# A two-layer graph network on one core: the last layer's bias added by one transfer for each stream, and seven orders changed on TensorE, ScalarE and VectorE

## The chip, the core and the metric

The kernel runs on one core of a Trainium2 chip. The metric is the time of the device in microseconds (us). A core has TensorE (matrix products), VectorE, ScalarE, GpSimd (POOL) and SyncE (SP). Each takes its instructions strictly in its program's order, and they are tied together by semaphores alone: an instruction that waits holds up all that stands behind it on its engine. Transfers (DMAs) are issued by SP and by POOL. The inputs and outputs are float32.

## The reference

`x` is (64, 128, 128): 64 batches of T = 128 nodes and D = 128 features. `adj` is 128 x 128. Cut to what matters:

```python
h = maximum(layernorm(x), 0)
# first layer: two graph convolutions, then windowed LSTMs
h = relu(adj @ (h @ Wg0 + bg0));  h = relu(adj @ (h @ Wg1 + bg1))      # for each batch
for p in 1, 2, 3, 4:               # skips: windows of p nodes through an LSTM, its last
    last = lstm_last(Wih[p-1], Whh[p-1], bih[p-1], bhh[p-1], windows(h, p))
    h[:, p-1::p, :] = last         # state replaces the window's last node
x = x + h
# last layer
h = maximum(layernorm(x), 0)
out = diag(adj) * (h @ W[0]) + triu(adj, 1) @ (h @ W[1]) + tril(adj, -1) @ (h @ W[2]) + bias
x = x + out
```

## The kernel before

The 64 batches are taken in 4 groups of 16 (`GROUPS`, `G`), and a group in 2 streams of 8 batches (`STREAMS`, `HB`). The LSTM of a group is a list of 22 units (`UNITS`, line 48), each one step of one window length for one stream: units 0 to 3 have p = 1, 4 to 7 p = 2, 8 to 13 p = 3, 14 to 21 p = 4. Even units are stream 0, odd ones stream 1. A unit's gates are I, C, O at the first step of a window and I, C, F, O after it. Every product is split in three passes for precision (line 596 high x high, 597 low weights x high, 605 high weights x low data; 624, 625 and 628 likewise for the recurrent product). The pass with the low data needs what VectorE writes last for a unit (`unit_low`, lines 1101 to 1107).

For each unit ScalarE makes the gates (line 915) and the tanh of the cell (930); VectorE makes the cell (`unit_cell`, 1029), the hidden state (`unit_hidden`, 1070) and its low part. PSUM has 8 banks, 4 for each stream, one for each gate.

The last layer of a group is computed during the LSTM of the next group. Its operands come turned around by transfers: POOL issues, for each stream, a 512 KB transfer that adds the LSTM's result to the turned x (line 469), then two transfers of 256 KB that add minus the mean (476), then the reciprocal deviation (`rstd`, 425), and after both streams one transfer of 1024 KB that adds the bias to the 16 batches of `X` (484, semaphore `bias_in`). The means themselves go through DRAM by SP (`spread_means`, 381). The last group is different: it has no such transfers, and its bias is added on POOL and VectorE.

A table written by hand (`START`, `START_F`, `STEADY`, `LATE`, lines 95 to 118) places the last layer's pieces between the LSTM's gates: a key (k, m) is "in unit k before its gate m", or after its gates if m is their number. The pieces on TensorE are VALUE n (the three products of batch n), SUM q (the two adjacency products of a quad of 4 batches) and a wait FORGET n. They use the bank of gate F, so F's products wait for what `START_F` names. On ScalarE `TURN_AT` places `turn_up(q)` (the relu of the turned x of quad q), and a VALUE is copied from PSUM there too. On VectorE three steps are placed by `START_MID` (after the unit's cell and before its hidden state), `START_BETWEEN` (after the hidden state) and `START_LATE` (after the low part): LOW q (`turn_down`, the low part of the turned x), OWN q (`add_own`, the diagonal term into `X`) and ADD q (`add_out`, the SUM into `X`). A number of -1 means quad 3 of the group one further back, and is left out if there is none. So in group 1 nothing with -1 runs; in groups 2 and 3 it does. `LN_STATS_AT` places the first layer norm's statistics of the next group.

OWN waits for the bias to be in `X`:

```python
        def add_own(g, q, lo=0, hi=PACK):
            dve.wait_ge(value_sb, G * g + q * PACK + hi)
            ...
                dve.wait_ge(bias_in, 16 * ((QUADS * g + q) // QUADS + 1))     # line 1170
```

Here g is the group whose last layer is done, one less than the group whose LSTM runs; QUADS = 4, HBANKS = 2, and a transfer adds 16 to its semaphore. `START_MID = {0: ((OWN, -1),), ...}` has OWN -1 in unit 0, between cell and hidden state.

Of the kernel before, what the change touches and what calls it, by code (L numbers as in the profile page):

```python
# [62 lines left out]
def last_unit(k, s):  # L63
# [37 lines left out]
         (8, 0): (Piece(VALUE, 8, 0, (VALUE, 7)),), (8, 3): (Piece(SUM, 1, 1, (FORGET, 7)),),  # L101
         (9, 3): (Piece(VALUE, 9, 0, (VALUE, 8)),), (10, 3): (Piece(VALUE, 10, 1, (SUM, 1)),),
# [43 lines left out]

LN_STATS_AT = {3: range(0, 3), 5: range(3, 5), 6: range(5, 9), 10: range(9, 12), 11: range(12, G)}
LN_COMBINE_AT = 11
# [11 lines left out]
def program(nc, x_tbd, x_dbt, adj_t, adj_diag, wg0, bg0_col, wg1, bg1, wih_t, whh_t, bih_t, bhh_t, w_l1, bias, bias_row, out_tbd):  # L160
    with ExitStack() as ctx:
# [116 lines left out]
        xt_summed = [sem(f"xt_summed{s}") for s in range(STREAMS)]  # L278
        xt_centred = [sem(f"xt_centred{q}") for q in range(QUADS)]
        means_out = [sem(f"means_out{s}") for s in range(STREAMS)]  # L280
        bias_in = sem("bias_in")
        turn_mm = sem("turn_mm")
# [70 lines left out]
        def _(sp):  # L353
# [34 lines left out]
            def store(i, quads):  # L388
                for q in quads:
                    pieces = END_PIECES if i == GROUPS - 1 and q == LAST else ((0, PACK),)  # L390
                    for n, (lo, hi) in enumerate(pieces):
                        if on_pool(i, q):
                            sp.wait_ge(pool_shifted, q + 1)
                        elif i == GROUPS - 1:
                            sp.wait_ge(shifted_x, shifts_to(q))
                        else:
                            sp.wait_ge(bias_in, 16 * (i + 1))
                        sp.wait_ge(out_ready, QUADS * i + q + 1 + n)
                        part = slice(i * G + q * PACK + lo, i * G + q * PACK + hi)
                        sp.dma_start(out_tbd[:, part, :], X[:, part, :]).then_inc(stored, 16)  # L400
# [16 lines left out]
        def _(pool):  # L417
# [42 lines left out]
            def group(i):  # L460
                if i == 0:
                    for s in range(STREAMS):
                        rstd(VE1, var1, 2 * (QUARTERS + s + 1), RS1, rs1, HB * s, HB * s + HB)
                else:
                    rstd(VE1, var1, 2 * (QUARTERS + i + 2), RS1, rs1, 0, G)
                pool.wait_ge(xt_in, 16 * (i + 1))
                for s in range(STREAMS):
                    pool.wait_ge(lstm_step, STEPS * i + STEPS_BEFORE[LAST_OF[s] + 1])
                    pool.dma_start(turned_stream(s), HF[:, s, :, :, :].rearrange("p c t e -> p (c t e)"),
                                   accum_op=ALU.add).then_inc(xt_summed[s], 16)  # L470
                for s in range(STREAMS):
                    pool.wait_ge(xt_summed[s], 16 * (i + 1))
                    pool.wait_ge(means_out[s], 16 * (i + 1))
                    for h in range(HBANKS):
                        part = slice(h * PACK * T, (h + 1) * PACK * T)
                        pool.dma_start(turned_stream(s)[:, part], MEANS[i, s, part].rearrange("(a n) -> a n", a=1).broadcast_to(
                            [128, PACK * T]), accum_op=ALU.add).then_inc(xt_centred[HBANKS * s + h], 16)
# [5 lines left out]
                part = slice(i * G, (i + 1) * G)  # L483
                pool.dma_start(X[:, part, :].rearrange("t b d -> t (b d)"), bias_row.rearrange("(a n) -> a n", a=1).broadcast_to(
                    [T, G * D]), accum_op=ALU.add).then_inc(bias_in, 16)

# [16 lines left out]
        def _(pe):  # L503
# [47 lines left out]
            def unit(k, i, plan):  # L551
# [24 lines left out]
                for m, q in enumerate(gates):  # L576
# [21 lines left out]
                    if j == 0 and p > 1 and plan is None:  # L598
                        continue
                    if prev is None and m == 0:  # L600

                        pe.wait_ge(h_low, 2 * HBANKS * i + HBANKS * (s + 1))
                    if j == 0 and p > 1 and m == 0:
                        pe.wait_ge(h_out, LOWS * i + prev + 1)
                    mm = pe.matmul(dst, WIH[:, p - 1, cols], x_low, start=False, stop=(j == 0))  # L605
                    if j == 0:
# [7 lines left out]
                if j > 0:  # L614

                    pe.wait_ge(lstm_step, STEPS * i + STEPS_BEFORE[prev] + STEPS_OF[prev])
                    for q in gates:
                        if i == GROUPS - 1 and k == LAST_OF[1] and q == gates[-1]:

                            pe.wait_ge(gate_act, GATES * i + GATES_BEFORE[LAST_OF[0]] + len(LATER_STEP))  # L620
                            transpose_h(0, i, range(PACK))
                        dst = bank(s, q)[:, 0:n]
                        cols = slice(q * D, q * D + D)
                        pe.matmul(dst, WHH[:, p - 2, cols], SH[:, s, 0:n], start=False, stop=False)  # L624
                        pe.matmul(dst, WHL[:, p - 2, cols], SH[:, s, 0:n], start=False, stop=False)  # L625
                        if q == gates[0]:
                            pe.wait_ge(h_out, LOWS * i + prev + 1)
                        pe.matmul(dst, WHH[:, p - 2, cols], SL[:, s, 0:n], start=False,  # L628
                                  stop=True).then_inc(gate_mm, 1)
# [176 lines left out]
        def _(act):  # L806
# [164 lines left out]
        def _(dve):  # L971
# [190 lines left out]
            def add_own(g, q, lo=0, hi=PACK):  # L1162
# [69 lines left out]
            def units(i, more, plan):  # L1232
                for k in range(len(UNITS)):
# [127 lines left out]
```

## Time and profile before

| what | value |
|---|---|
| median of 3 runs | 403.95 us (403.22 to 404.17) |
| the profiled execution's own time | 402.31 us |
| its span | 400.1 us |
| TensorE busy | 390.5 us (98%) |
| VectorE busy | 335.8 us (84%) |
| ScalarE busy | 281.1 us (70%) |
| POOL busy | 63.9 us (16%) |
| moved by DMA | 23.78 MB |

Busy and idle times are those of one execution. The groups' LSTMs begin at about 24, 107, 200 and 297 us of the span. A row of a timeline gives the start and the duration in us, the engine, the line, output <- inputs with shapes, and in brackets how long the engine was idle before it and what ended that. In the views matmuls overlap (a 512-column pass is shown as 0.39 us, but one starts every 0.23 us). POOL's rows of an issue last as long as it writes the transfer's descriptors; the data follows.

### The profile page before, as it was taken

To read this page: it belongs to the slowest core of one execution; us is meant where nothing else is said; L and a number is where in the kernel's file an instruction comes from. 1 tells how busy PE (TensorE), PEld (TensorE's weight loads), DVE (VectorE), ACT (ScalarE), POOL (GpSimd) and SP (SyncE) were. 2 spreads that over 40 slices of the span, in tenths; PEclk is the share of its full clock that TensorE was granted. 3 is DMA by queue.
4 is the path that set the end of the run, shared out by engine and by line. 5 is a ranking of instruction groups with operands and counts; after the bars stand their busy time and mean duration, and the time that the engine had idled before them with its cause. 6 is when DMAs were issued, how large, how long until landed. Compare 5 with 4: busy or idle time off the path is not lost.

```text
span 400.1 us, 6501 instructions
## 1 busy us (share of the span) xinstructions
PE 390.5 (98%) x2346; PEld 339.4 (85%) x2346; DVE 335.8 (84%) x868; ACT 281.1 (70%) x555; POOL 63.9 (16%) x65
## 2 busy tenths in 40 slices
PE   7999999999999999999999799999999999999997
PEld 7787889998976889899877579999897788989886
DVE  6569999998998788797997678989798958787897
ACT  4768777875697777776499477676669867667554
POOL 4910200101340003001151000300134000000250
PEclk9999999999999999999999999999999999999999
DMA  7860000005364000204158000030527400000003
GB/s 208 304 252 2 0 0 2 2 0 106 53 93 94 0 28 0 92 41 80 29 80 157 27 2 27 2 131 2 107 27 131 108 0 28 0 28 1 2 1 131
DMA packets 12127, 23.78 MB, mean 59 GB/s; under 512 B 4672, under 2 KB 6080, under 8 KB 10816
## 3 DMA queue, kind: packets, MB, share of 16 engines
q0 software_dynamic: 3024, 9.44, 13.6%
q1 hardware_dynamic: 9072, 13.94, 10.1%
q8 instruction: 18, 0.29, 0.3%
q14 instruction: 13, 0.11, 0.1%
HBM read 16.01 MB, written 4.22 MB: 51 GB/s over the span
## 4 chain that ended last, share of the span: by engine, by line
PE 44%; DVE 29%; DMA 12%; ACT 9%; issue 3%; POOL 2%; SPq 0%; DVEq 0%; POOLq 0%; ACTq 0%
DMA X<-bias_row 8%; PE PS L596 6%; PE PS L605 6%; PE PS L597 6%; PE PS L628 4%; ACT GT L915 4%; PE PS L624 4%; PE PS L625 4%; DMA means<-MINUS 4%; PE PS L666 3%; DVE CS L1058 3%; DVE IC L1040 3%; ACT TC L930 2%; DVE ST L1121 2%; DVE CS L1050 2%
## 5 line engine op out<-in xcount | busy, mean ns | idle before, releaser
L915 ACT ACTIVATE GT<-PS,BG 128x256 f32<-128x256 f32 (+2 forms) x312 | 158.2, 563 | 17.0 <-PE PS L628 14.2
L596 PE MATMUL PS<-HH,WIH 128*128 128x256 f32 (+2 forms) x312 | 106.6, 342 | 2.5 <-DVE X L1182 2.4
L597 PE MATMUL PS<-HH,WIL 128*128 128x256 f32 (+2 forms) x312 | 102.7, 330 | 0.0
L605 PE MATMUL PS<-HL,WIH 128*128 128x256 f32 (+2 forms) x294 | 97.4, 331 | 0.6
L930 ACT ACTIVATE TC<-CS 128x512 f32<-128x512 f32 (+2 forms) x88 | 44.9, 510 | 48.2 <-DVE CS L1058 33.2
L596 PEld LDWEIGHTS PS<-HH,WIH 128*128 128x128 f32 x312 | 58.7, 188 | 12.9 <-DVE HH L1099 4.2
L428 POOL TENSOR_TENSOR RS<-VE,NHALF 128x4 f32<-128x4 f32 (+2 forms) x18 | 34.7, 1926 | 210.0 <-DVE VE L994 140.5
L597 PEld LDWEIGHTS PS<-HH,WIL 128*128 128x128 f32 x312 | 58.8, 188 | 4.0 <-issue 1.2
L605 PEld LDWEIGHTS PS<-HL,WIH 128*128 128x128 f32 x294 | 55.5, 189 | 7.1 <-DVE HL L1107 2.5
L628 PE MATMUL PS<-SL,WHH 128*128 128x256 f32 (+2 forms) x192 | 60.2, 313 | 0.2
L624 PE MATMUL PS<-SH,WHH 128*128 128x256 f32 (+2 forms) x192 | 60.0, 312 | 0.0
L625 PE MATMUL PS<-SH,WHL 128*128 128x256 f32 (+2 forms) x192 | 59.7, 311 | 0.0
L1040 DVE TENSOR_TENSOR IC<-GT 128x256 f32<-128x256 f32 (+2 forms) x48 | 23.8, 496 | 21.7 <-ACT GT L915 21.5
L628 PEld LDWEIGHTS PS<-SL,WHH 128*128 128x128 f32 x192 | 36.2, 189 | 2.2 <-DVE SL L1107 0.8
L624 PEld LDWEIGHTS PS<-SH,WHH 128*128 128x128 f32 x192 | 36.3, 189 | 1.5 <-DVE SH L1099 0.2
L625 PEld LDWEIGHTS PS<-SH,WHL 128*128 128x128 f32 x192 | 36.3, 189 | 1.3
L1095 DVE TENSOR_TENSOR HT<-GT,TC 128x256 f32<-128x256 f32 (+2 forms) x48 | 23.7, 495 | 7.5 <-ACT TC L930 6.5
L1095 DVE TENSOR_TENSOR HF<-GT,TC 128x512 f32<-128x512 f32 (+2 forms) x32 | 18.9, 591 | 8.1 <-ACT TC L930 7.5
L1037 DVE TENSOR_TENSOR CS<-GT 128x512 f32<-128x512 f32 (+2 forms) x40 | 23.8, 596 | 1.8 <-ACT GT L915 1.6
L1107 DVE TENSOR_TENSOR SL<-HT,SH 128x256 fp32r<-128x256 f32 (+2 forms) x48 | 23.9, 497 | 1.5
L1058 DVE TENSOR_TENSOR CS<-IC,CS 128x256 f32<-128x256 f32 (+3 forms) x48 | 23.4, 488 | 1.6
L658 PE MATMUL PS<-WLH,HTH 128*128 128x384 f32 x64 | 23.4, 366 | 1.3 <-DVE HTL L1152 0.6
(99 smaller groups left out, 640.1 us busy)
## 6 DMA issues: line engine op xcount, KB each, us to landing
out_tbd<-X SPq DMA_DIRECT2D x15, 256.0 KB, 2.0
X<-x_tbd SPq DMA_DIRECT2D x3, 1024.0 KB, 12.9
H<-x_dbt SPq DMA_DIRECT2D x3, 1024.0 KB, 6.1
H<-HF POOLq DMA_DIRECT2D x6, 512.0 KB, 4.7
H<-means POOLq DMA_DIRECT2D x12, 256.0 KB, 5.0
X<-bias_row POOLq DMA_DIRECT2D x3, 1024.0 KB, 9.8
WI<-wih_t SPq DMA_DIRECT2D x1, 1024.0 KB, 5.5
X<-x_tbd SPq DMA_DIRECT2D x3, 256.0 KB, 3.5
```

The costliest lines, as they stand in the source:

```text
L428: pool.tensor_tensor(rs[:, lo:hi], ve[:, lo:hi], NHALF[:, lo:hi], ALU.pow).then_inc(done, 1)
L596: pe.matmul(dst, WIH[:, p - 1, cols], x_high, start=True, stop=False)
L597: pe.matmul(dst, WIL[:, p - 1, cols], x_high, start=False, stop=False)
L605: mm = pe.matmul(dst, WIH[:, p - 1, cols], x_low, start=False, stop=(j == 0))
L624: pe.matmul(dst, WHH[:, p - 2, cols], SH[:, s, 0:n], start=False, stop=False)
L625: pe.matmul(dst, WHL[:, p - 2, cols], SH[:, s, 0:n], start=False, stop=False)
L628: pe.matmul(dst, WHH[:, p - 2, cols], SL[:, s, 0:n], start=False, stop=True).then_inc(gate_mm, 1)
L915: act.activation(GT[:, s, q, 0:n], bank(s, q)[:, 0:n], ACT.Tanh if q == C else ACT.Sigmoid, bias=BG[:, 4 * (p - 1) + q:4 * (p - 1) + q + 1 ...
L930: act.activation(TC[:, s, done:n], CS[:, s, done:n], ACT.Tanh).then_inc(tanh_ready, 1)
L1040: dve.tensor_tensor(IC[:, s, 0:n], GT[:, s, I, 0:n], GT[:, s, C, 0:n], ALU.mult).then_inc(lstm_step, 1)
L1058: dve.tensor_tensor(CS[:, s, half:n], IC[:, s, half:n], CS[:, s, half:n], ALU.add).then_inc(cell_ready, 1)
L1095: dve.tensor_tensor(full, o, tc, ALU.mult).then_inc(lstm_step, 1)
```

## The change

POOL's bias transfer of 1024 KB becomes two of 512 KB, one for each stream, each with a semaphore of its own. That of stream 0 is issued as soon as stream 0's statistics have been taken (`bn2`), ahead of the transfers of the means; that of stream 1 after the second `rstd`. The two transfers of 256 KB of means for each stream become one of 512 KB. The waits are rewritten accordingly, in `store`, `turn_up` and `add_own`. In the tables: VALUE 9 moves from after unit 9's gates to before its gate O; the relu `turn_up(2)` from before unit 6's VALUE 5 copy to after it; ADD -1 in unit 1 from after to before the hidden state; ADD 1 from unit 9 to unit 8; the next group's statistics of batches 0 to 4 from the middle of units 3 and 5 to the end of unit 5. In units 8 and 15 of groups 1 to 3 the low pass of the first gate is issued with that of the second gate; in units 10 and 16 of group 0 and unit 16 of group 3 the same is done for the recurrent low pass.

```diff
-         (9, 3): (Piece(VALUE, 9, 0, (VALUE, 8)),), (10, 3): ...
+         (9, 2): (Piece(VALUE, 9, 0, (VALUE, 8)),), (10, 3): ...
-TURN_AT = {(1, 1): 0, (4, 1): 1, (6, 0): 2, (10, 0): 3}
+TURN_AT = {(1, 1): 0, (4, 1): 1, (6, 2): 2, (10, 0): 3}
-START_BETWEEN = {0: ((LOW, 0),), 1: ((ADD, -1),), 14: ((ADD, 2),)}
-START_MID = {0: ((OWN, -1),), 4: ((LOW, 1),), 5: ((ADD, 0),), 7: ((OWN, 1),), 9: ((ADD, 1),), 12: ((OWN, 2),)}
+START_BETWEEN = {0: ((LOW, 0),), 14: ((ADD, 2),)}
+START_MID = {0: ((OWN, -1),), 1: ((ADD, -1),), 4: ((LOW, 1),), 5: ((ADD, 0),), 7: ((OWN, 1),), 8: ((ADD, 1),), 12: ((OWN, 2),)}
+LOWS_TOGETHER = (8, 15)
-LN_STATS_AT = {3: range(0, 3), 5: range(3, 5), 6: range(5, 9), 10: range(9, 12), 11: range(12, G)}
+LN_STATS_LATE_AT = {5: range(0, 5)}
+LN_STATS_AT = {6: range(5, 9), 10: range(9, 12), 11: range(12, G)}
...
# SP, store
-                            sp.wait_ge(bias_in, 16 * (i + 1))
+                            sp.wait_ge(bias_in[q // HBANKS], 16 * (i + 1))
# POOL, group(i)
+                def stream_bias(s):
+                    pool.wait_ge(bn2, G * i + HB * (s + 1))
+                    part = slice(i * G + s * HB, i * G + (s + 1) * HB)
+                    pool.dma_start(X[:, part, :].rearrange("t b d -> t (b d)"),
+                                   bias_row.rearrange("(a n) -> a n", a=1).broadcast_to([T, HB * D]),
+                                   accum_op=ALU.add).then_inc(bias_in[s], 16)
+                stream_bias(0)
                 for s in range(STREAMS):
                     pool.wait_ge(xt_summed[s], 16 * (i + 1))
                     pool.wait_ge(means_out[s], 16 * (i + 1))
-                    for h in range(HBANKS):
-                        ...                      # two transfers, xt_centred[HBANKS * s + h]
+                    pool.dma_start(turned_stream(s), MEANS[i, s, :]...,
+                                   accum_op=ALU.add).then_inc(xt_centred[s], 16)
                     ...
                     rstd(VE2, var2, 2 * STREAMS * i + 2 * s + 2, RS2, rs2, HB * s, HB * s + HB)
-                pool.wait_ge(bn2, G * (i + 1))
-                ...                              # one transfer for 16 batches, bias_in
+                stream_bias(1)
# TensorE, unit: with a plan, in units 8 and 15
+                    if plan and k in LOWS_TOGETHER and m == 0:
+                        continue
-                    if j == 0 and p > 1 and m == 0:
+                    if j == 0 and p > 1 and m == (1 if k in LOWS_TOGETHER else 0):
                         pe.wait_ge(h_out, LOWS * i + prev + 1)
+                    if k in LOWS_TOGETHER and m == 1:
+                        ...                      # the first gate's low pass, then_inc(gate_mm, 1)
+                        together = (plan is None and k in (10, 16)) or (i == GROUPS - 1 and k == 16)
...
# ScalarE, turn_up
-                    act.wait_ge(xt_centred[q], 16 * (g + 1))
+                    act.wait_ge(xt_centred[q // HBANKS], 16 * (g + 1))
# VectorE, add_own
-                    dve.wait_ge(bias_in, 16 * ((QUADS * g + q) // QUADS + 1))
+                    dve.wait_ge(bias_in[q // HBANKS], 16 * (g + 1))
# VectorE, units, after plan.late
+                    if more and plan and k in LN_STATS_LATE_AT:
+                        stats1(i + 1, LN_STATS_LATE_AT[k])
```

## Rows read from the trace of the kernel before

**Rows 1.** The page's first lines: span, then busy us, share and instructions of TensorE.
```profile
span 400.1 us, 6501 instructions
PE 390.5 (98%) x2346; PEld 339.4 (85%) x2346; DVE 335.8 (84%) x868; ACT 281.1 (70%) x555; POOL 63.9 (16%) x65
```

**Rows 2.** The page's slices: TensorE's granted clock, tenths of full speed.
```profile
PEclk9999999999999999999999999999999999999999
```

**Rows 3.** The page's chain that ended last, shares of the span by line.
```profile
DMA X<-bias_row 8%; PE PS L596 6%; PE PS L605 6%; PE PS L597 6%; PE PS L628 4%; ACT GT L915 4%; PE PS L624 4%; PE PS L625 4%; DMA means<-MINUS 4%; PE PS L666 3%; DVE CS L1058 3%; DVE IC L1040 3%; ACT TC L930 2%; DVE ST L1121 2%; DVE CS L1050 2%
```

**Rows 4.** The same chain in order of time: start us, us, what.
```profile
200.53 5.53 DMA means<-MINUS
...
208.36 1.08 POOL RS L428
209.44 11.82 DMA X<-bias_row
...
305.86 9.80 DMA X<-bias_row
```

**Rows 5.** POOL's timeline, the issues of the means in groups 0, 1, 2.
```profile
104.26 1.76 POOL L476 DMA_DIRECT2D H<-means  x2 [9.55 <-DMA means<-MINUS]
...
206.56 1.80 POOL L476 DMA_DIRECT2D H<-means  x2 [4.81 <-DMA means<-MINUS]
...
302.97 1.96 POOL L476 DMA_DIRECT2D H<-means  x2 [3.39 <-DMA means<-MINUS]
```

**Rows 6.** The page's DMA issues: count, KB each, median us to landing.
```profile
H<-HF POOLq DMA_DIRECT2D x6, 512.0 KB, 4.7
H<-means POOLq DMA_DIRECT2D x12, 256.0 KB, 5.0
```

**Rows 7.** Line 385 alone, the six transfers of 4 KB of means.
```profile
DMA to landing us min/median/max: 3.1/4.6/5.5
```

**Rows 8.** VectorE's timeline, start of groups 2 and 3.
```profile
202.69 0.75 DVE L1173 SCALAR_TENSOR_TENSOR X<-WH,DIAG,X 128x512 f32<-128x512 f32 x1
...
204.61 0.68 DVE L1152 SCALAR_TENSOR_TENSOR HTL<-H,HTH 128x512 fp32r<-128x512 f32 x1
...
205.82 0.68 DVE L1107 TENSOR_TENSOR HL<-HF,HH 128x512 fp32r<-128x512 f32 x1
...
207.87 0.68 DVE L1182 TENSOR_TENSOR X<-PS,X 128x512 f32<-128x512 f32 x1
...
221.36 0.75 DVE L1173 SCALAR_TENSOR_TENSOR X<-WI,DIAG,X 128x512 f32<-128x512 f32 x1 [2.66 <-DMA X<-bias_row]
...
223.23 0.48 DVE L975 BATCH_NORM_STATS2 ST<-X 128x6 f32<-128x128 f32 x2
...
228.07 0.69 DVE L1040 TENSOR_TENSOR IC<-GT 128x512 f32<-128x512 f32 x1 [1.98 <-ACT GT L915]
...
299.56 0.75 DVE L1173 SCALAR_TENSOR_TENSOR X<-WH,DIAG,X 128x512 f32<-128x512 f32 x1
...
315.76 0.75 DVE L1173 SCALAR_TENSOR_TENSOR X<-WI,DIAG,X 128x512 f32<-128x512 f32 x1 [0.16 <-DMA X<-bias_row]
```

**Rows 9.** TensorE's timeline in group 2: VALUE 0, VALUE 1, unit 6's gate F.
```profile
207.01 0.34 PE L658 MATMUL PS<-WLH,HTH 128*128 128x384 f32 x1
...
208.60 0.45 PE L658 MATMUL PS<-WLH,HTH 128*128 128x384 f32 x1 [0.20 <-DVE X L1182]
...
223.37 0.50 PE L596 MATMUL PS<-HH,WIH 128*128 128x512 f32 x1 [2.40 <-DVE X L1182]
```

**Rows 10.** ScalarE's timeline in group 1: `turn_up(0)`.
```profile
109.88 0.62 ACT L851 ACTIVATE HTH<-H 128x512 fp32r<-128x512 f32 x1
```

**Rows 11.** Waits of weight loads: us in total, times, longest.
```profile
PEld PS L605 <- DVE HL L1107: 2.5, 7, 0.4
...
PEld PS L658 <- DVE X L1182: 2.1, 5, 0.7
...
PEld PS L628 <- DVE SL L1107: 0.8, 3, 0.3
```

More of the change, by code:

```diff
@@ L101 @@
          (8, 0): (Piece(VALUE, 8, 0, (VALUE, 7)),), (8, 3): (Piece(SUM, 1, 1, (FORGET, 7)),),
-         (9, 3): (Piece(VALUE, 9, 0, (VALUE, 8)),), (10, 3): (Piece(VALUE, 10, 1, (SUM, 1)),),
+         (9, 2): (Piece(VALUE, 9, 0, (VALUE, 8)),), (10, 3): (Piece(VALUE, 10, 1, (SUM, 1)),),
          (11, 3): (Piece(VALUE, 11, 0, (FORGET, 10)),), (14, 3): (Piece(SUM, 2, 1, (FORGET, 13)),)}
-TURN_AT = {(1, 1): 0, (4, 1): 1, (6, 0): 2, (10, 0): 3}
+TURN_AT = {(1, 1): 0, (4, 1): 1, (6, 2): 2, (10, 0): 3}
 START_F = {6: (SUM, 0), 7: (VALUE, 6), 10: (VALUE, 9), 11: (VALUE, 10), 12: (VALUE, 11)}
-START_BETWEEN = {0: ((LOW, 0),), 1: ((ADD, -1),), 14: ((ADD, 2),)}
-START_MID = {0: ((OWN, -1),), 4: ((LOW, 1),), 5: ((ADD, 0),), 7: ((OWN, 1),), 9: ((ADD, 1),), 12: ((OWN, 2),)}
+START_BETWEEN = {0: ((LOW, 0),), 14: ((ADD, 2),)}
+START_MID = {0: ((OWN, -1),), 1: ((ADD, -1),), 4: ((LOW, 1),), 5: ((ADD, 0),), 7: ((OWN, 1),), 8: ((ADD, 1),), 12: ((OWN, 2),)}
 START_LATE = {4: ((OWN, 0),), 5: ((LOW, 2),), 9: ((LOW, 3),)}
@@ L278, in program @@
         xt_summed = [sem(f"xt_summed{s}") for s in range(STREAMS)]
-        xt_centred = [sem(f"xt_centred{q}") for q in range(QUADS)]
+        xt_centred = [sem(f"xt_centred{s}") for s in range(STREAMS)]
         means_out = [sem(f"means_out{s}") for s in range(STREAMS)]
-        bias_in = sem("bias_in")
+        bias_in = [sem(f"bias_in{s}") for s in range(STREAMS)]
         turn_mm = sem("turn_mm")
@@ L473, in group @@
                     pool.wait_ge(means_out[s], 16 * (i + 1))
-                    for h in range(HBANKS):
-                        part = slice(h * PACK * T, (h + 1) * PACK * T)
-                        pool.dma_start(turned_stream(s)[:, part], MEANS[i, s, part].rearrange("(a n) -> a n", a=1).broadcast_to(
-                            [128, PACK * T]), accum_op=ALU.add).then_inc(xt_centred[HBANKS * s + h], 16)
+                    pool.dma_start(turned_stream(s), MEANS[i, s, :].rearrange("(a n) -> a n", a=1).broadcast_to(
+                        [128, HB * T]), accum_op=ALU.add).then_inc(xt_centred[s], 16)
                     if i > 0:
@@ L481, in group @@
                     rstd(VE2, var2, 2 * STREAMS * i + 2 * s + 2, RS2, rs2, HB * s, HB * s + HB)
-                pool.wait_ge(bn2, G * (i + 1))
-                part = slice(i * G, (i + 1) * G)
-                pool.dma_start(X[:, part, :].rearrange("t b d -> t (b d)"), bias_row.rearrange("(a n) -> a n", a=1).broadcast_to(
-                    [T, G * D]), accum_op=ALU.add).then_inc(bias_in, 16)
+                stream_bias(1)
             for i in range(GROUPS - 1):
@@ L599, in unit @@
                         continue
+                    if plan and k in LOWS_TOGETHER and m == 0:
+                        continue
                     if prev is None and m == 0:
                         pe.wait_ge(h_low, 2 * HBANKS * i + HBANKS * (s + 1))
-                    if j == 0 and p > 1 and m == 0:
+                    if j == 0 and p > 1 and m == (1 if k in LOWS_TOGETHER else 0):
                         pe.wait_ge(h_out, LOWS * i + prev + 1)
+                    if k in LOWS_TOGETHER and m == 1:
+                        first = gates[0]
+                        pe.matmul(bank(s, first)[:, 0:n].rearrange("p (w b) -> p w b", b=HB),
+                                  WIH[:, p - 1, first * D:first * D + D], x_low, start=False, stop=True).then_inc(gate_mm, 1)
                     mm = pe.matmul(dst, WIH[:, p - 1, cols], x_low, start=False, stop=(j == 0))
@@ L625, in unit @@
                         pe.matmul(dst, WHL[:, p - 2, cols], SH[:, s, 0:n], start=False, stop=False)
-                        if q == gates[0]:
+                        if together and q == gates[0]:
+                            continue
+                        if q == gates[1 if together else 0]:
                             pe.wait_ge(h_out, LOWS * i + prev + 1)
+                        if together and q == gates[1]:
+                            first = gates[0]
+                            pe.matmul(bank(s, first)[:, 0:n], WHH[:, p - 2, first * D:first * D + D], SL[:, s, 0:n],
+                                      start=False, stop=True).then_inc(gate_mm, 1)
                         pe.matmul(dst, WHH[:, p - 2, cols], SL[:, s, 0:n], start=False,
@@ L1348 @@
         "bias": a["L1_gnn_bias"],
-        "bias_row": np.broadcast_to(a["L1_gnn_bias"], (G, D)).reshape(G * D),
+        "bias_row": np.broadcast_to(a["L1_gnn_bias"], (HB, D)).reshape(HB * D),
     }
```

## The prediction

> **What bounds the kernel now.** I read the page's busy times first: TensorE is busy 390.5 of 400.1 us [rows 1], so whatever makes TensorE wait is added to the time, and there are at most some 10 us to gain. Its granted clock is at its full level, 2.4 GHz, in every slice [rows 2]. Then the chain of waits: its largest line is the bias transfer, 8% of the span [rows 3], in stretches of 9.80 and 11.82 us [rows 4]. Such a share says that the chain runs through the transfer, not that removing it frees so much: TensorE works beside it. What the transfer costs stands in the timelines. In group 2 VectorE comes to OWN 0 and is idle 2.66 us until the bias has landed [rows 8]; TensorE then finds unit 6's gate F blocked (it waits for ADD 0, behind OWN 0) and is idle 2.40 us [rows 9]. In group 3 the same wait is 0.16 us [rows 8]. So the intended prize is about 2.5 us, and a few tenths elsewhere [rows 11].
>
> **The new wait.** The part that decides is one line of `add_own`, so I follow its index. OWN -1 runs in groups 2 and 3 between cell and hidden state of unit 0, with q = -1 and g = i - 1. Before, (4g - 1) // 4 + 1 is g: it asks for 16g, the bias of the group two back, landed 78 us before in group 3 (221.26 in the chain, OWN -1 at 299.56) [rows 4, 8]. After, -1 // 2 is -1, so it takes the last semaphore, that of stream 1, and asks for 16(g + 1): the second bias transfer of group g itself, which at that time isn't even issued. It is no deadlock: POOL issues that transfer without anything that VectorE has still to do. But VectorE stands at OWN -1, which began at 202.69 and 299.56 without a wait [rows 8], until the landing, which I call T2 and T3. Behind it on VectorE are the hidden state of unit 0, LOW 0, cell 1 and all else; ScalarE finishes the gates of unit 1 and stops at the tanh of cell 1; TensorE does units 0 and 1, SUM -1 and two gates of unit 2, and stops at VALUE 0, at 207.01 before [rows 9], which needs LOW 0. In group 1 there is no OWN -1 and no such wait.
>
> **When the transfer lands.** Before, POOL began to issue the second stream's means at 206.56 and 302.97 [rows 5], two issues in 1.80 and 1.96, so 0.9 for one. After, one issue is left. The chain has 1.08 from the end of the issue to the next one, for the reciprocal deviation [rows 4]. So the second bias is issued at 206.56 + 0.9 + 1.08 = 208.5, and at 302.97 + 1.98 = 304.95. A 512 KB transfer of the same kind lands 4.7 after its issue [rows 6]. Alone it would land at 213.2 and 309.65: the lower bound. Behind the means' 512 KB, issued 2.0 earlier and itself needing 4.7, it is up to 2.7 later: 215.9 and 312.35. The upper bound is the landing of today, 221.26 and 315.66 [rows 4]. I take T2 = 215.5 and T3 = 311.9, near the middle value, since the two transfers share the same engines and the means may be a little late (below).
>
> The Trainium skill, DMA: Bandwidth & Descriptors, section "Anatomy of one DMA — SWDGE (gpsimd) path", fits a transfer issued by GpSimd as 2.0 us plus its bytes at 436 GB/s, which is 3.2 us for 512 KB. The row of this case has 4.7 (these transfers add to what is there), so the measurement is used; by the page's fit both landings would come some 3 us sooner and the sum below would be some 6 us less.
>
> **From the landing to the time.** From OWN -1 at 202.69 VectorE needed until 205.3 to have LOW 0 done (204.61 + 0.68), until 206.5 for the low part of unit 0, and ADD -1 takes 0.6 more when it stands right there, as after the change [rows 8]. VALUE 1 needs ADD -1, so it starts at T2 + 4.5, against 208.60 before: TensorE is late by T2 - 204.1. VectorE is late by T2 - 202.7, which is 1.4 more. Units 0 to 5 leave it nearly no idle time, so that doesn't shrink, but for some 0.4 from ADD -1's new place and the statistics that leave units 3 and 5. At OWN 0 the old wait of 2.66 is gone, as that needs only the first bias transfer, and stream 0's was issued long before. VectorE then carries T2 - 205.8; TensorE, whose 2.40 is gone too, would have T2 - 206.5; the later one decides, since unit 6's gate F waits for ADD 0. Group 2: 215.5 - 205.8 = 9.7. In group 3 the wait at OWN 0 was only 0.16: T3 - 299.56 - 0.16 - 0.4 = T3 - 300.1, which is 11.8. After unit 6 TensorE is the bound, at 98%, and nothing can give the delay back. Sum +21.5.
>
> **The other parts.** (a) The first bias transfer, 512 KB, is issued when stream 0's statistics are done, some 0.5 us before the 4 KB write of the means and in its way. The shortest of these writes takes 3.1, the one beside another transfer 5.53 [rows 4, 7]. That would make stream 0's means up to 2 us late. They were issued at 104.26 in group 1 [rows 5], so the first relu, at 109.88 [rows 10], which now needs the whole 512 KB (4.7 from the issue) [rows 6], has from 0.9 us of cover to 1.1 us of stall. Bounds -0.2 to +1.5, taken +0.5, for group 1 alone; in the others the new stall covers it. (b) Two instead of one low pass behind the wait, in units 8 and 15 and in the recurrent units: at most what stands in the rows, 2.5 + 0.8 [rows 11]; many of these stalls are in other units, so -1.4. (c) ADD 1 one unit earlier, VALUE 9 and the relu of quad 2 moved: VALUE waits for an ADD 2.1 in all [rows 11], a part of it in these places: -0.6. ADD 1 stands behind SUM 1, which is done by then, and VectorE is waiting for a tanh there. (d) The statistics at the end of unit 5 fall into VectorE's idle time of 1.98 us before the cell of unit 6: five at 0.24 each, 1.2, cost nothing; without that cover they would cost as much as they did in units 3 and 5 [rows 8]. (b) and (c) could also bring nothing, or cost a few tenths where the first gate comes later to ScalarE: together between -3.0 and +0.5, taken -2.0. (e) TensorE's idle time in the new stall, from 207.0 to T2 + 2.6, is some 11 us, where the longest shown before a matmul is 2.40 [rows 9]. If its clock falls in it, a 512-column pass takes 0.46 for 0.23 afterwards; 1.4 us of that are covered by VectorE being later. With 4 us at the lower level that is 0.6 a stall: +1 for both; bounds 0 and the rival below.
>
> Sum: 402.3 + 21.5 + 0.5 - 2.0 + 1.0 = 423.3 for an execution like the profiled one. The median of the runs shown is 1.6 above that one (403.95 against 402.31), so **425.0**.
>
> **Rivals.** (1) The stall isn't there: the semaphore is met in time, or something covers it. This is the other side. The point from which it decides is a landing before 202.7, and the issue alone is later than that. Then group 2 gains 2.4, the rest -1.5: 402.3 - 3.9 + 1.6 = 400. For it: all other edits aim at a real wait. Against it: the index above. (2) Splitting doesn't bring the second landing forward: same bytes on the same engines, landing at 221.3 and 315.7 as now. That adds 5.8 + 3.8 = 9.6: 434.6. Against it: 0.5 MB of 1.5 are gone from behind the means, and the stores of finished quads stand still in the stall. (3) TensorE's clock falls and stays low. No row of this trace shows a fall: even after 2.40 us of idleness it is at the upper level [rows 2, 9]. With 12 us at the lower level in each of two stalls it loses 6.0 - 1.4 = 4.6 a stall instead of the 0.5 counted: 433. A rule of the Trainium skill speaks for this one: TensorE: Matmul & The Clock Gate, section "What's actually happening", has 1.2 GHz as the default and says that activity releases it, so an idle TensorE comes back slow.
>
> **How the numbers follow.** Forecast 0.75, rival 1 0.06, rival 2 0.07, rival 3 0.12. The forecast's own bounds: both landings at their lower bound take 2.3 + 2.25 off and (b, c) one more, 419; to the other side 1 us later each, and 1 each from (a) and (b, c), 429. The range that leaves 2 in 10 out takes in part of rivals 2 and 3: 417 to 434. A difference under 0.3% can't be told from none in this kernel. Only rival 1 gives faster or the same: faster 0.05, same 0.01, slower 0.94.
>
> **What would show it.** In the changed kernel's profile: in groups 2 and 3 OWN -1 (line of `add_own`) idle before it by 10 to 13 us, ended by the bias transfer; none in group 1, whose length stays within 1.5 us of before. The hole in TensorE 8 to 12 us before VALUE 0, twice, and its busy share down to about 93%. No idle time before OWN 0. The granted clock in the slices after each hole tells (e) and rival 3. The issue and landing of the second bias transfer tell T2, T3 and rival 2. The prediction is wrong if OWN -1 doesn't wait, or if later units make up the delay, which would show as group 2 being less than 8 us longer with the stall in place.

## The result, and the profile after

The changed kernel takes **423.4 us** (median of 4 runs, 422.63 to 424.24) against 404.06 for the kernel before in the same comparison: a ratio of 1.0478 (95% interval 1.0444 to 1.0513). 425.0 was predicted, with a range of 417 to 434. The profiled execution took 424.01, its span is 422.3. In the comparisons of the experiments some executions of the kernel before (6 of 23, 6 of 17 and 4 of 11) ran slower at a lower mean clock than the rest, and the ratios and its medians leave them out.

The page of the changed kernel, its first lines and its slices (against rows 1 and 2 of before: [rows 1], [rows 2]):

```profile
span 422.3 us, 6498 instructions
...
PE 391.8 (93%) x2346; PEld 343.9 (81%) x2346; DVE 335.5 (79%) x868; ACT 281.2 (67%) x555; POOL 61.1 (14%) x62
...
PE   8999999999899999999629999999972999999996
...
PEclk9999999999999999999959999999996999999999
```

No engine has much more work: TensorE is busy 391.8 us where it was 390.5, VectorE 335.5 where it was 335.8. The span is 22.2 us longer and nearly all of that is idle time, and the slices (10.6 us each) say where it lies: two holes on TensorE, in the slices from 201 and 306 us, that is at the start of the LSTMs of groups 2 and 3. The second slice of each hole, in which TensorE begins again, has a lower clock. The shape of the loss is thus known before any wait is looked at: it isn't spread, it is at two places.

The largest waits of the changed kernel (engine, line, what it waited for: us in total, times, longest):

```profile
DVE X L1194 <- DMA X<-bias_row: 26.2, 2, 13.5
PEld PS L679 <- DVE HTL L1173: 25.3, 3, 12.1
PE PS L679 <- DVE HTL L1173: 24.6, 5, 11.6
...
ACT HTH L872 <- DMA H<-means: 7.1, 3, 3.0
```

The first three are one chain, seen from VectorE and from TensorE's weight loads and products: `add_own` (now line 1194) waits for the bias, `turn_down` (1173) stands behind it on VectorE, and VALUE 0 (679) waits for that. They must not be added up. The fourth is another matter, and will be needed later. VectorE's timeline of the changed kernel at the start of groups 2 and 3 (against [rows 8]):

```profile
202.64 0.69 DVE L1058 TENSOR_TENSOR CS<-GT 128x512 f32<-128x512 f32 x1
216.87 0.75 DVE L1194 SCALAR_TENSOR_TENSOR X<-WH,DIAG,X 128x512 f32<-128x512 f32 x1 [13.53 <-DMA X<-bias_row]
...
218.60 0.69 DVE L1173 SCALAR_TENSOR_TENSOR HTL<-H,HTH 128x512 fp32r<-128x512 f32 x1
...
220.41 0.68 DVE L1203 TENSOR_TENSOR X<-PS,X 128x512 f32<-128x512 f32 x1
...
232.42 0.74 DVE L1194 SCALAR_TENSOR_TENSOR X<-WI,DIAG,X 128x512 f32<-128x512 f32 x1
...
322.59 0.75 DVE L1194 SCALAR_TENSOR_TENSOR X<-WH,DIAG,X 128x512 f32<-128x512 f32 x1 [12.69 <-DMA X<-bias_row]
...
338.19 0.74 DVE L1194 SCALAR_TENSOR_TENSOR X<-WI,DIAG,X 128x512 f32<-128x512 f32 x1
```

OWN -1 had no idle time before it and has 13.53 and 12.69 us. OWN 0, at 232.42 and 338.19, had 2.66 and 0.16 and has none. LOW 0 (218.60) begins 1.73 us after OWN -1, where it was 1.92; ADD -1 (220.41) begins 3.54 us after it, where it was 5.18, since it has moved ahead of unit 1's hidden state. POOL's timeline and the chain, for when the second bias is issued and lands (against [rows 4], [rows 5]):

```profile
209.10 0.92 POOL L485 DMA_DIRECT2D H<-means  x1 [7.09 <-DMA means<-MINUS]
...
314.65 0.92 POOL L485 DMA_DIRECT2D H<-means  x1 [5.20 <-DMA means<-MINUS]
```

```profile
201.07 7.52 DMA means<-MINUS
...
211.36 5.41 DMA X<-bias_row
...
316.91 5.58 DMA X<-bias_row
```

The 4 KB write of stream 1's means took 7.52 us where it took 5.53, so POOL came to the means later. The bias then landed 5.4 to 5.6 us after its issue. TensorE in the hole and after it, from its timeline and from the windows (busy us of each engine, granted clock, DMA share, GB/s), against [rows 9]:

```profile
219.34 0.69 PE L679 MATMUL PS<-WLH,HTH 128*128 128x384 f32 x1 [11.63 <-DVE HTL L1173]
...
221.75 0.52 PE L679 MATMUL PS<-WLH,HTH 128*128 128x384 f32 x1
```

```profile
209.00:210.00 1.00, 0.00 (x0) 0.00 (x0) 0.00 (x0) 0.34 (x1) 0.90 (x2) 0.88 0.00 0
210.00:211.00 1.00, 0.00 (x0) 0.00 (x0) 0.00 (x0) 0.00 (x0) 1.00 (x2) 0.50 0.64 57
...
222.00:223.00 1.00, 1.00 (x4) 1.00 (x4) 1.00 (x3) 0.97 (x3) 0.00 (x0) 0.50 0.69 262
223.00:224.00 1.00, 1.00 (x5) 0.77 (x5) 0.90 (x2) 0.96 (x3) 0.00 (x0) 0.80 0.00 0
```

In the hole the granted clock goes to 0.50, which is 1.2 GHz, and it stays there until TensorE has worked again for some 4 us. VALUE 1 begins at 221.75, 0.66 us after ADD -1 was done (221.09), and waits for nothing but the products ahead of it.

### The profile page after: what moved, and what is told of

The parts are those of the page before. It is cut to its first block, busy times and chain, and to the rows that moved or that the text cites. A ratio compares the mean times of both kernels' runs of the same rounds, so it can differ in the third digit from the quotient of the medians.

```text
span 422.3 us, 6498 instructions
## 1 busy us (share of the span) xinstructions
PE 391.8 (93%) x2346; PEld 343.9 (81%) x2346; DVE 335.5 (79%) x868; ACT 281.2 (67%) x555; POOL 61.1 (14%) x62
## 4 chain that ended last, share of the span: by engine, by line
PE 50%; DVE 26%; ACT 9%; DMA 9%; issue 3%; POOL 1%; SPq 0%; DVEq 0%; POOLq 0%; ACTq 0%
PE PS L602 7%; PE PS L603 7%; PE PS L618 7%; ACT GT L936 5%; DMA means<-MINUS 4%; PE PS L638 4%; PE PS L649 4%; PE PS L639 4%; PE PS L687 3%; PE PS L679 3%; DMA X<-bias_row 3%; DVE CS L1079 2%; DVE IC L1061 2%; PE PS L680 2%; PE PS L681 2%
## 5 line engine op out<-in xcount | busy, mean ns | idle before, releaser
L936 ACT ACTIVATE GT<-PS,BG 128x256 f32<-128x256 f32 (+2 forms) x312 | 158.5, 563 | 16.3 <-PE PS L649 12.2
L618 PE MATMUL PS<-HL,WIH 128*128 128x256 f32 (+2 forms) x288 | 95.8, 333 | 0.4
L430 POOL TENSOR_TENSOR RS<-VE,NHALF 128x4 f32<-128x4 f32 (+2 forms) x18 | 32.6, 1811 | 231.0 <-DVE VE L1015 148.5
L649 PE MATMUL PS<-SL,WHH 128*128 128x256 f32 (+2 forms) x189 | 59.0, 312 | 0.0
L679 PEld LDWEIGHTS PS<-WLH,HTH 128*128 128x128 f32 x64 | 12.8, 201 | 29.2 <-DVE HTL L1173 25.3
L1194 DVE SCALAR_TENSOR_TENSOR X<-WH,DIAG,X 128x512 f32<-128x512 f32 (+1 forms) x9 | 6.1, 688 | 26.3 <-DMA X<-bias_row 26.2
```

What stands on the lines that cost most here:

```text
L430: pool.tensor_tensor(rs[:, lo:hi], ve[:, lo:hi], NHALF[:, lo:hi], ALU.pow).then_inc(done, 1)
L679: pe.matmul(dst, high, w_high, start=True, stop=False)
L936: act.activation(GT[:, s, q, 0:n], bank(s, q)[:, 0:n], ACT.Tanh if q == C else ACT.Sigmoid, bias=BG[:, 4 * (p - 1) + q:4 * (p - 1) + q + 1 ...
```

## The experiments

There were three comparisons: experiments 1, 2, 3 and 10 in the first, 4 to 7 in the second, 8, 9 and 11 in the third. The medians of the kernel before in them were 403.51, 403.21 and 403.66. Its single times scatter by some 1% to either side, so the ratios have intervals of 0.3 to 0.7% to either side; kernels of one comparison are better set against each other by their own medians, which scatter less. A difference taken from one comparison to another (experiment 1 against 5, 6 or 7; 7 against 8 or 9; the changed kernel against any but 11) is less sure: by medians and by ratios it comes out up to some 1 us apart. The edits of experiments 1, 3, 5, 6 and 10 are shown against the changed kernel.

**1. The changed kernel with only OWN -1's count mended.**

```diff
-                    dve.wait_ge(bias_in[q // HBANKS], 16 * (g + 1))
+                    dve.wait_ge(bias_in[q // HBANKS], 16 * (g + 1 + q // QUADS))
```

> The changed kernel with one count mended: OWN -1 asks for the bias of its own group, 16(g + 1 + q // QUADS), which for q = -1 is 16g; nothing else. Theory W (the new wait of OWN -1 makes the whole loss): the idle time of 13.5 and 12.7 us before OWN -1 is gone, the granted clock is 1.00 throughout, and the time falls by 18 to 24 us from 423.4 to 399 to 405. Within that, theory L (the first bias transfer makes the means of stream 0 late, so the first relu of each group waits 1.6 to 3.0 us on ScalarE, which the big stall had covered in groups 2 and 3) says 401 to 405, that is no faster than before; without L the kernel would be at 399 to 401. The rival (splitting and moving the transfers costs the time, not the count): stays above 415.

401.65 us (400.09 to 402.46), ratio 0.9966 (0.9938 to 0.9994): 21.8 us below the changed kernel by the medians, some 21 by the ratios. The bias is no longer among the waits, and no other change was undone. So the whole loss is this one count. But of the intended gain only 0.3% is there, and the relus wait as theory L has it. One part of theory W missed: the clock wasn't at 1.00 throughout (more at the end). The waits and ScalarE's timeline of this experiment (against [rows 10]):

```profile
ACT HTH L872 <- DMA H<-means: 6.5, 3, 2.3
```

```profile
112.29 0.63 ACT L872 ACTIVATE HTH<-H 128x512 fp32r<-128x512 f32 x1 [2.33 <-DMA H<-means]
...
207.54 0.63 ACT L872 ACTIVATE HTH<-H 128x512 fp32r<-128x512 f32 x1 [1.95 <-DMA H<-means]
...
302.54 0.63 ACT L872 ACTIVATE HTH<-H 128x512 fp32r<-128x512 f32 x1 [2.24 <-DMA H<-means]
```

In each group ScalarE now stands for 2 us before the first relu, which had no idle time before.

**2. The kernel before with only that count changed.**

```diff
-                    dve.wait_ge(bias_in, 16 * ((QUADS * g + q) // QUADS + 1))
+                    dve.wait_ge(bias_in, 16 * (g + 1))
```

> The kernel before with one count changed: OWN -1 asks for the bias of the next group, 16(g + 1), of the one undivided transfer; all transfers and orders are the old ones. Theory W: the same stall as in the changed kernel, but until the old landing, 221.3 and 315.7 plus the delay of group 2. By the prediction's own rule (landing less 205.8 and less 300.1) that is 15.5 + 15.6 = 31 us, and some 1 us for the clock: 434 to 438. The rival (the split transfers cost the time): within 1% of 404.

438.47 us (437.84 to 440.73), ratio 1.0907 (1.0842 to 1.0972). The count alone, on the old transfers, makes more than the whole loss. So the split transfers aren't needed for it. The changed kernel is 15 us faster than this one: its bias lands sooner (it stands at OWN -1 until 216.87 and not until 221.73), and it has the seven orders, which are worth some 3 to 4 us (below). The waits of this experiment, and its clock after the first hole:

```profile
DVE X L1173 <- DMA X<-bias_row: 35.3, 3, 18.6
```

```profile
221.73 0.75 DVE L1173 SCALAR_TENSOR_TENSOR X<-WH,DIAG,X 128x512 f32<-128x512 f32 x1 [18.57 <-DMA X<-bias_row]
```

```profile
231.00:232.00 1.00, 1.00 (x5) 0.99 (x4) 0.03 (x1) 0.69 (x1) 0.00 (x0) 0.50 0.00 0
232.00:233.00 1.00, 1.00 (x4) 0.83 (x3) 1.00 (x4) 0.58 (x1) 0.00 (x0) 0.62 0.00 0
```

The bias waits grew by 35.3 - 3.0 = 32.3 us; the span grew by 36.5. What is over, some 4 us, is the clock as far as I can see: here it stayed at 0.50 until 232, 8 us after TensorE had begun again, and VectorE came to wait for gates in that time. That this is all of the 4 us wasn't tested.

**3. New transfers with the mended count, old orders.** The tables are those of the kernel before, and no low passes are joined.

```diff
...
-TURN_AT = {(1, 1): 0, (4, 1): 1, (6, 2): 2, (10, 0): 3}
+TURN_AT = {(1, 1): 0, (4, 1): 1, (6, 0): 2, (10, 0): 3}
...
-LOWS_TOGETHER = (8, 15)
+LOWS_TOGETHER = ()
...
-                        together = (plan is None and k in (10, 16)) or (i == GROUPS - 1 and k == 16)
+                        together = False
...
```

> The new transfers with the mended count of OWN -1, and all orders as before (VALUE 9, the relu of quad 2, ADD -1, ADD 1, the statistics, the low passes one by one). It is the first experiment without the seven orders. If the orders bring the 2.0 us of the prediction: 2 us above the first. If they bring nothing: the same. Theory L: 403 to 407, with ScalarE idle 1.6 to 3.0 us before the first relu in each of groups 1 to 3.

406.03 us (403.4 to 408.01), ratio 1.0072 (1.0036 to 1.0108). Even with the right count the new transfers by themselves make the kernel slower, with 6.3 us of waits before the first relus. Beside experiment 1, in the same comparison, the orders are worth 4.4 us, where 2.0 were expected. Its profiled execution also has some 3 us at the lower clock, from 213 to 216.

**4. The orders alone, on the old transfers.** The edit is the part of the change's diff in the tables, in `unit` and in `units`, with nothing of the transfers.

> The seven orders alone, on the transfers and the bias waits of the kernel before (one bias transfer of 1024 KB after the means, means in transfers of 256 KB, OWN -1 asking for 16g). The prediction had -2.0 us for the orders. With the new transfers and the mended count the orders were worth 4.4 us (406.03 without, 401.65 with). If they are worth the same here: 399.5; if the prediction's figure is right and the rest was their covering of the late relu: 401 to 402; ScalarE has no idle time before the first relus. The OWN 0 wait of 2.7 us in group 2 stays.

401.58 us (398.43 to 404.09), ratio 0.9973 (0.9937 to 1.0008): not to be told from no change. VectorE's timeline of this experiment shows where a part of the gain goes:

```profile
125.86 0.75 DVE L1190 SCALAR_TENSOR_TENSOR X<-WI,DIAG,X 128x512 f32<-128x512 f32 x1 [1.89 <-DMA X<-bias_row]
...
222.16 0.75 DVE L1190 SCALAR_TENSOR_TENSOR X<-WI,DIAG,X 128x512 f32<-128x512 f32 x1 [3.07 <-DMA X<-bias_row]
```

VectorE comes earlier to OWN 0 and waits there for the same landing: 5.9 us in all, where the kernel before has 3.0. TensorE's timeline and the windows show another part in this execution:

```profile
224.17 0.79 PE L598 MATMUL PS<-HH,WIH 128*128 128x512 f32 x1 [2.82 <-DVE X L1199]
```

```profile
223.00:224.00 1.00, 0.00 (x0) 0.00 (x0) 1.00 (x2) 0.46 (x1) 0.00 (x0) 0.72 0.00 0
...
229.00:230.00 1.00, 1.00 (x4) 0.71 (x4) 0.00 (x0) 0.63 (x1) 0.00 (x0) 0.50 0.00 0
```

The hole behind OWN 0 is 2.82 us, where it was 2.40, and this time the clock fell to its lower level and stayed there for some 6 us of work. The three executions at a mean clock of 1.00 have a median of 400.03, the nine below it 401.85. So what the orders are worth here is mixed with the clock, and that they need the early first bias is likely and not shown by this experiment alone.

**5. As experiment 1, the means again in two transfers.**

```diff
...
-                    pool.dma_start(turned_stream(s), MEANS[i, s, :]..., accum_op=ALU.add).then_inc(xt_centred[s], 16)
+                    for h in range(HBANKS):
+                        part = slice(h * PACK * T, (h + 1) * PACK * T)
+                        pool.dma_start(turned_stream(s)[:, part], MEANS[i, s, part]..., accum_op=ALU.add).then_inc(xt_centred[HBANKS * s + h], 16)
...
-                    act.wait_ge(xt_centred[q // HBANKS], 16 * (g + 1))
+                    act.wait_ge(xt_centred[q], 16 * (g + 1))
...
```

> The changed kernel with the mended count of OWN -1 and the means again in two transfers of 256 KB a stream, each quad's relu waiting for its own. Against the first experiment (401.65 us, ScalarE idle 2.3, 2.0 and 2.2 us before the first relus). Theory L1 (the merging makes the relu late): the idle times fall by some 1.0 to 1.5 us each, the time to 398 to 400. Theory L2 (the first bias transfer, ahead, makes the means late): the idle times shrink by under 0.7 us, the time stays above 400.5.

397.52 us (396.13 to 398.21), ratio 0.9838 (0.9796 to 0.988). The idle times before the first relus are 0.41, 1.16 and 1.07 us.

**6. As experiment 1, each bias after its stream's means.**

```diff
-                stream_bias(0)
                 for s in range(STREAMS):
                     ...
                     rstd(VE2, var2, 2 * STREAMS * i + 2 * s + 2, RS2, rs2, HB * s, HB * s + HB)
-                stream_bias(1)
+                    stream_bias(s)
```

> The changed kernel with the mended count of OWN -1 and each stream's bias transfer issued after its means and reciprocal deviation, so that nothing is in the way of stream 0's means; the means stay one transfer of 512 KB. Theory L2 (the first bias transfer makes the means late): POOL issues stream 0's means 0.5 to 1 us sooner, the idle times before the first relus fall from 2.0 to 2.3 to under 1.2, the time to 398 to 400. Theory L1: they stay at 1.5 us and more, the time above 400.5. The first bias then moves beside stream 1's means write, which may land later; VALUE 4 and what follows have 5 us of cover for that.

397.31 us (395.88 to 399.38), ratio 0.9836 (0.9784 to 0.9888). Neither theory alone: against experiment 1 each cure takes 4.1 to 4.3 us by the medians, some 5 by the ratios. The waits before the first relus, in experiment 5 and then in experiment 6:

```profile
ACT HTH L874 <- DMA H<-means: 2.6, 3, 1.2
```

```profile
ACT HTH L871 <- DMA H<-means: 2.8, 3, 1.2
```

Both fall from 6.5 us to under 3. The merging makes the relu wait for bytes that it doesn't read; the bias ahead makes both the 4 KB write and the transfer of the means later. In group 1 the means are issued at 105.04 with the bias ahead and at 104.49 without, and the relu begins 7.25 and 6.15 us after that. Each cost about as much.

**7. Both together.**

> Both of the two before this one together: mended count, means in two transfers, each bias after its stream's means. If the first relus' waits are what is left of the change's cost, they go to 0 to 0.5 us and the kernel is the fastest of all: 396.5 to 398.5, 1.3 to 1.8% below the kernel before. The rival: the first bias transfer now sits ahead of stream 1's means and delays the second bias; OWN 0 needs only the first, so nothing more than 0.5 us should come of it; if something does, 399 to 401.

**395.29 us** (395.04 to 395.6), ratio 0.9788 (0.9749 to 0.9827): the fastest kernel, 2.1% below the one before, and a little faster than was expected of it. Its page:

```profile
span 393.3 us, 6504 instructions
...
PE 387.2 (98%) x2346; PEld 340.6 (87%) x2346; DVE 335.4 (85%) x868; ACT 280.3 (71%) x555; POOL 67.0 (17%) x68
```

Neither the means nor the bias is among the waits of ScalarE or VectorE any more. The two cures overlap, 4.1 + 4.3 against 6.4 us together, since either already takes away a part of the wait that the other would.

**8. Experiment 7 without the joined low passes.** The edit is that of `LOWS_TOGETHER` and `together` in experiment 3.

> The fastest kernel so far (mended count, means in two transfers, each bias after its stream's means; 395.29 us) without the joined low passes of units 8 and 15 and of the recurrent units 10 and 16. The prediction valued them at 1.4 us: 396.7. If their waits were hidden in the overlapping weight loads: 395.3. If they carry most of the orders' worth (4.4 us between the two kernels with a late first relu): 398 or more.

396.17 us (395.8 to 396.38), ratio 0.9798 (0.9751 to 0.9846): 0.9 us above by the medians, 0.4 by the ratios.

**9. Experiment 7 with all seven orders as before.**

> The same fastest kernel with none of the seven orders changed, so only the transfers are new. The first relu isn't late here, so this is the worth of the orders by themselves. The prediction's term is 2.0 us: 397.3. The difference of 4.4 us that was seen with a late relu: 399.7. Neither: the same as with them, 395.3.

398.63 us (398.42 to 399.0), ratio 0.9861 (0.9818 to 0.9904): 3.3 us above experiment 7 by the medians, 2.9 by the ratios. Of that the moved additions, relu, VALUE 9 and statistics have 2.5 (against experiment 8, in the same comparison), and the low passes what is left, 0.4 to 0.9. The new transfers, with the right count and both cures, gain 1.4% without any of the orders. In the waits of this experiment TensorE's loads wait for an ADD 1.8 us in all:

```profile
PEld PS L680 <- DVE X L1204: 1.8, 5, 0.5
```

It is gone in experiment 7.

**10. TensorE kept busy in the holes of the changed kernel.**

```diff
+                if n == 0 and g in (1, 2) and g < GROUPS - 1:
+                    for n_fill in range(45):
+                        pe.matmul(ps[:, 0:T], ONES[:, :], ONES[:, :], start=True, stop=True)
                 if b == 0:
                     pe.wait_ge(turn_low, QUADS * g + q + 1)
```

> The changed kernel with 45 idle products (128 x 128 of ones, some 0.21 us each, 9.6 us in all) put ahead of VALUE 0 in groups 2 and 3, into the bank that VALUE 0 then overwrites. They fill most of TensorE's holes of 11.6 and 10.8 us and are over before VALUE 0 may start. If the lower clock after the hole costs what the rows show at VALUE 1 (221.75 where ADD -1 was done at 221.09), the gain is 0.6 us a stall, 1 to 1.5 in all: 422 to 422.5. If the half clock costs all of its some 4 us of products, 2 us a stall: 419 to 420. The granted clock is 1.00 in both. If the clock costs nothing: 423.4.

421.76 us (420.41 to 422.25), ratio 1.0476 (1.043 to 1.0522), the same ratio as the changed kernel's in another comparison. The span was 420.3 against 422.3. That left open whether the clock costs anything; experiment 11 has both kernels in one comparison.

**11. The changed kernel again, and the filled one again beside it.**

> The changed kernel itself, unaltered, beside the next one on the same chip: 422 to 425 us, granted clock 0.97.

> The changed kernel with 45 idle products in each of TensorE's two holes, once more, now beside the changed kernel itself. The first time its profile's span was 2.0 us shorter, but the ratio to the kernel before was the same. If the lower clock after a hole costs the prediction's 0.5 us a stall, it is 1 us below the changed kernel; if it costs 1 us a stall, as the spans had it, 2 us below; if the difference was scatter, none.

423.0 us (421.96 to 424.94) and 422.0 us (420.57 to 422.85). TensorE's timeline of the filled kernel (each of the 45 products is two of its records):

```profile
208.45 10.21 PE L678 MATMUL PS<-ONES 128*128 128x128 f32 x90
220.09 0.45 PE L684 MATMUL PS<-WLH,HTH 128*128 128x384 f32 x1 [1.43 <-DVE HTL L1178]
221.90 0.45 PE L684 MATMUL PS<-WLH,HTH 128*128 128x384 f32 x1 [0.31 <-DVE X L1208]
```

The fill takes 10.21 us of the hole, and after it VALUE 1 waits for ADD -1, as it didn't in the changed kernel. 1.0 us for two holes, but the single times overlap; that agrees with the term in sign and size and proves neither.

## Why the prediction was right, point by point

**The new wait.** Right in place, count and consequence, and this carries the prediction: it came from following the index -1 through `q // HBANKS` and `16 * (g + 1)`. Experiments 1 and 2 show it from both sides: take the count away and 21.8 us go, put it alone into the kernel before and 35.0 us come.

**When the transfer lands.** The landings were nearly right (T2 = 215.5 predicted, 216.8 measured of which 0.56 is group 1's own delay; T3 = 311.9, and 322.5 less the 10.3 that the groups ahead had lost by then is 312.2), but by two errors that cancel, and that part is luck. The second bias was to be issued at 208.5 and 304.95; it was issued at 211.36 and 316.91, which is 2.3 and 1.7 us late after the same shifts. The step that failed held stream 1's means to be on time but for "a little"; with the transfers of stream 0 changed, their 4 KB write in group 2 took 7.52 us instead of 5.53. And the flight was to be 7.0 us, behind the means; it was 5.4 and 5.6. That is nearer to the row of a transfer alone (4.7) than to the middle value taken. The estimate of 3.2 us for 512 KB by the fit of the Trainium skill (DMA: Bandwidth & Descriptors, section "Anatomy of one DMA — SWDGE (gpsimd) path"), which the prediction set aside, doesn't hold for these accumulating transfers here either; in the changed kernel the two kinds of 512 KB have medians of 7.0 and 6.0 from issue to landing:

```profile
X<-bias_row POOLq DMA_DIRECT2D x6, 512.0 KB, 7.0
H<-means POOLq DMA_DIRECT2D x6, 512.0 KB, 6.0
```

**From the landing to the time.** The arithmetic of delays held. The chain has stream 0's low parts (line 1045, before 1024) near the end of each group; first the changed kernel, then the kernel before:

```profile
199.44 1.19 DVE HL L1045 x2
...
306.02 1.19 DVE HL L1045 x2
```

```profile
198.88 1.19 DVE HL L1024 x2
...
295.75 1.19 DVE HL L1024 x2
```

Those two places, and the ends, show group 1 late by 0.56 us, group 2 by another 9.7 and group 3, with the end, by another 11.9. At OWN 0, where the prediction has its two delays, they can be read directly: 232.42 against 221.36 and 338.19 against 315.76, less what the groups ahead had lost, is 10.5 and 12.2. The prediction's rule gives 10.4 and 12.1 from the measured landings. It had 9.7 and 11.8, from its own. That nothing gives a delay back after unit 6 was not quite so: 0.8 and 0.2 us were gone again at the end of the groups. The orders of units 8 and 15, a term of their own in the prediction, stand there; that it was they is an argument.

**(a) The first bias in the way of the means.** Right in place and mis-sized. Group 1's relu waited 1.64 us, above the 1.1 that its own reasoning gave. The means weren't up to 2 us late: they were issued at 104.69 instead of 104.26. What it had wrong is the transfer itself, taken at 4.7 us:

```profile
104.69 6.88 DMA H<-means
```

The group was late by only 0.56, near the 0.5 taken, but not by the sum that gave the 0.5; that the orders took the rest back there is likely and wasn't tried. The prediction said that the big stall covers it in the other groups, and so it was. What it didn't draw from that is what the term costs once the stall is mended: 6.4 us, more than the whole prize of about 2.5, by experiments 1 and 7. That includes the merging of the means, which the term counted too.

**(b), (c) The orders.** Predicted -2.0, measured -3.3 (experiment 9; -2.9 by the ratios). The low passes were over-valued, 1.4 for 0.9 or less. The moved steps were under-valued, 0.6 for 2.5: the term counted TensorE's waits for an ADD alone, 1.8 us of which do go. VectorE has next to no idle time in the units where these steps stand, so a step taken out of the way there may be worth its whole length; that is an argument, and which of the moves carries the 2.5 was not tried.

**(d) The statistics.** At the end of unit 5 the five stand at 236.87, and VectorE is still idle 0.90 us before the next cell (238.83): covered, as said.

**(e) The clock.** With TensorE idle the granted clock went to 0.50. It returned after some 4 us of work, which is the value that the prediction took without a row that showed one, and the cost of 1 us is what experiments 10 and 11 suggest. The rule of the Trainium skill in rival 3 (TensorE: Matmul & The Clock Gate, section "What's actually happening"), that activity releases the clock from 1.2 GHz, agrees with this trace. Rival 3 itself, 12 us at the lower level, is refuted for this kernel, but experiment 2 has 8 us of it.

**The sum** was 21.5 + 0.5 - 2.0 + 1.0 = 21.0 against a span that grew by 22.2 and medians that differ by 19.3. The terms with what they measured: waits for the bias 26.2 - 3.0 = 23.2, the first relu 1.6, the orders -3.3, the clock 1.0, together 22.5. Waits of one execution stand there beside differences of medians, so the close sum proves none of them. For an execution like the profiled one 423.3 was predicted and 424.01 measured. The prediction added 1.6 to that, by which the median of before lies above its profiled execution; the median of the changed kernel lies 0.6 below its own, and so 1.6 below the prediction.

**The rivals.** Rival 1 (no stall) was wrong; experiment 1, which is just that kernel, has 401.65 where rival 1 had 400. Rival 2 (the second landing no earlier) was wrong: the bias landed at 216.8 and not at 221.3.

## What to carry to other kernels

When a semaphore is split into a list, follow every index and every count through the edges of the loop, -1 above all: a count that asks for too much left the results right here, and only the profile shows it, as one long wait on an engine that had none there. Split transfers by who needs the bytes first and issue them in that order; a transfer moved ahead of a short, urgent one is paid for by everything behind that one. And set changes that touch one wait against each other both ways: the orders alone gained nothing that could be told from the scatter, the transfers alone, as the change has them, lost 0.7%, the transfers with the means ahead of the bias and in two pieces gained 1.4%, and with the orders 2.1%.

## What the runs showed of the hardware that wasn't expected

The clock can fall after a short hole, and a hole of the same length can leave it alone. Before, a hole of 2.40 us on TensorE had no effect on it [rows 2, 9]. In experiment 1 there was a fall after one of 2.36 us. TensorE's timeline and the windows of that experiment:

```profile
113.70 0.45 PE L679 MATMUL PS<-WLH,HTH 128*128 128x384 f32 x1 [2.36 <-DVE HTL L1173]
```

```profile
113.00:114.00 1.00, 0.30 (x2) 0.30 (x3) 1.00 (x2) 1.00 (x2) 0.88 (x2) 1.00 0.00 0
114.00:115.00 1.00, 1.00 (x5) 0.90 (x5) 0.86 (x2) 0.79 (x3) 1.00 (x2) 0.67 0.64 57
115.00:116.00 1.00, 1.00 (x4) 0.81 (x4) 0.94 (x2) 1.00 (x3) 1.00 (x2) 0.50 0.68 127
```

There it fell when TensorE was at work again, and stayed low for 3 us. In experiment 4 it fell near the end of the hole of 2.82 us, before the work, and in the filled kernel of experiment 11 in group 1's hole of 2.50 us, before the work too. Other holes left it alone: 1.62 us in group 1 of experiment 4, and 2.14 us in group 1 of the changed kernel's profile in experiment 11. What tells the holes apart stays open.

Such a fall doesn't come in every execution of a kernel, and it is a part of the scatter. Of experiment 1's twelve executions seven have a mean clock of 0.999 or 1.00 and five of 0.996 to 0.998. Of the kernel before's 35 that count in the three comparisons, 17 have 0.999 or 1.00, with a median of 401.64 us, and 18 less, with 403.94. The fastest kernel, which has no hole of even 1 us in its profile, has 1.00 in all six. So some part of its 2.1% is the clock that doesn't fall; against the 401.64 it is 1.6%. That the falls of the kernel before come at its hole of 2.40 us wasn't seen, as its profiled execution has none.

A write of 4 KB took between 3.1 and 5.5 us before [rows 7] and up to 7.52 after, with the same bytes. What had changed is what moves beside it; which of those transfers holds it up wasn't singled out.
